# One hybrid transformer layer on eight cores: reciprocal square roots as exp(-0.5 ln x), and semaphore waits in place of pipeline drains

## The reference, cut to what matters

```python
x = x + attn_a(layernorm(x))      # differential attention, 8 heads, cosine logits
x = x + ffn(layernorm(x))         # x @ int4-like(kernel) + bias + (x @ a) @ b
x = x + attn_b(layernorm(x))      # 16 heads, RoPE, causal softmax
x = x + ffn(layernorm(x))

def layernorm(x): return (x - mean(x)) / sqrt(var(x) + 1e-5)
def l2norm(t):    return t / maximum(norm(t, axis=-1), 1e-6)
# attn_a, per head; q1, q2, k1, k2 are 64 wide, v 128 wide
L1 = l2norm(q1) @ l2norm(k1).T * cos_scale
L2 = l2norm(q2) @ l2norm(k2).T * cos_scale
G  = tanh(delta_gain * (L1 - L2))
y  = (softmax(L1 + G) - lambda_full * softmax(L2 - G)) @ v
y  = y * rsqrt(mean(y * y) + 1e-5) * subln_weight * 0.5
```

## Time and profile before

| what | value |
|---|---|
| median of 3 runs | 7120.11 us (7112.32 to 7128.64) |
| the profiled execution's own time | 7132.85 us |
| its span, slowest core (7) | 7131.2 us; the cores 7099.8 to 7131.2 |
| mean granted TensorE clock, by core | 0.605 to 0.609 of full speed |
| busy, share of the span | PE 40%, DVE 43%, ACT 19%, POOL 5% |

### The profile page before, as it was taken

The page is one execution under the profiler, slowest core; times in us unless marked ns, Lnnn a source line. Parts: engine busy times, 40 slices in busy tenths (PEclk is TensorE's granted clock), DMA queues, the critical chain, the costliest instruction groups (busy, mean ns, idle before and its releaser), DMA issues.

```text
span 7131.2 us, 34446 instructions; the slowest of 8 cores (7099.8 to 7131.2 us)
## 1 busy us (share of the span) xinstructions
PE 2824.4 (40%) x8352; PEld 684.9 (10%) x8352; DVE 3100.4 (43%) x3605; ACT 1389.2 (19%) x1544; POOL 358.5 (5%) x655
## 2 busy tenths in 40 slices
PE   0013011065656542030265656551505564565615
PEld 0000000010101000000010101010101111111201
DVE  1334525335555545435145555534145344444341
ACT  0000000033444330000044444410000242033100
POOL 0100010100000000000000000000000000000000
PEclk9975555555555555555555555565857666766758
DMA  2000000000000000000000000000000000000001
GB/s 79 25 12 18 1 21 2 12 13 6 6 6 6 6 11 10 6 17 1 23 5 6 6 6 6 6 27 12 13 25 24 14 6 15 25 5 6 26 12 60
DMA packets 129374, 104.56 MB, mean 15 GB/s; under 512 B 62078, under 2 KB 111486, under 8 KB 126878
## 3 DMA queue, kind: packets, MB, share of 16 engines
q1 hardware_dynamic: 81726, 65.43, 3.0%
q0 software_dynamic: 47456, 36.93, 2.1%
HBM read 90.85 MB, written 11.11 MB: 14 GB/s over the span
## 4 chain that ended last, share of the span: by engine, by line
DVE 31%; DMA 22%; PE 19%; issue 12%; ACT 10%; DVEq 6%; ACTq 0%; POOLq 0%; SPq 0%; PEldq 0%
DVE a_pL L102 6%; PE pj_p L102 6%; DVEq L102 6%; DVE rrow L102 5%; DMA rnb<-scrb 4%; ACT a_E L102 4%; ACT a_G L102 4%; DVE rrbq L102 3%; PE f_p L102 2%; DVE tmpf L102 2%; DMA b_rb<-scrb 2%; DVE a_rrb L102 2%; DMA wqb<-qout 2%; PE tm_pv L102 2%; DMA rrow<-scr 2%
## 5 line engine op out<-in xcount | busy, mean ns | idle before, releaser
L102 DVE TENSOR_TENSOR a_pL<-a_pL,a_G 128x512 f32<-128x512 f32 x1024 | 664.3, 694 | 978.4 <-ACT a_G L102 956.7
L102 PE MATMUL a_pY<-a_E,aV 128*128 128x512 bf16 x1024 | 518.8, 610 | 747.0 <-ACT a_E L102 747.0
L102 ACT ACTIVATE a_E<-a_pL,ccol 128x1024 bf16<-128x1024 f32 x512 | 570.6, 1114 | 1119.4 <-DVE a_pL L102 1119.1
L102 PE MATMUL pj_p<-xnA,pj_wb 128*128 128x512 bf16 x512 | 210.0, 585 | 837.6 <-DVE pj_wb L102 837.6
L102 ACT ACTIVATE b_E<-b_pS,ccol 128x1024 bf16<-128x1024 f32 (+1 forms) x320 | 312.1, 985 | 753.2 <-PE b_pS L102 751.5
L102 ACT ACTIVATE a_G<-a_pD,gvec 128x512 bf16<-128x512 f32 x512 | 348.6, 681 | 87.3 <-PE a_pD L102 87.3
L102 ACT ACTIVATE rrow<-rrow 1x1024 f32<-1x1024 f32 x64 | 67.5, 1055 | 1499.2 <-DMA rrow<-scr 1499.2
L102 PE MATMUL a_pD<-aQ,aKn 128*128 128x512 bf16 x512 | 307.9, 601 | 67.0 <-ACT rrow L102 49.8
L102 PE MATMUL tm_pv<-tm_wvh,xnA 128*128 128x512 bf16 x256 | 59.7, 398 | 683.2 <-DVE tm_wvh L102 683.2
L102 PE MATMUL a_pL<-aQ,aK 64*128 64x512 bf16 x1024 | 310.3, 603 | 2.8 <-DVE aV L102 2.8
L102 ACT ACT_TABLE_LOAD x69 | 88.5, 1283 | 1115.5 <-PE a_pD L102 390.9
(11 more groups left out here) (145 smaller groups left out, 3372.3 us busy)
## 6 DMA issues: line engine op xcount, KB each, us to landing
resid<-xT SPq DMA_DIRECT2D x8, 1024.0 KB
qf<-fker SPq DMA_DIRECT2D x16, 512.0 KB
rnb<-scrb POOLq DMA_DIRECT2D x64, 128.0 KB, 4.9
a_rb<-scrb POOLq DMA_DIRECT2D x32, 256.0 KB, 3.6
pj_wf<-WqkT SPq DMA_DIRECT2D x32, 256.0 KB
out<-resid SPq DMA_DIRECT2D x8, 1024.0 KB, 10.2
pj_wf<-WqT SPq DMA_DIRECT2D x16, 256.0 KB
bbR<-scr POOLq DMA_DIRECT2D x16, 256.0 KB, 3.4
```

The lines of the kernel that those rows point to most:

```text
L102: r = getattr(eng, name)(*args, **kw)
```

## The change

Two things change. First, `1/sqrt(x)` is made otherwise in two places: in the LayerNorm row (16 steps) and in the norm step (64 steps). ScalarE now takes `AF.Ln` and then `AF.Exp` with scale -0.5 in place of `AF.Sqrt`, and DVE's reciprocal goes; the guard becomes a minimum with 1e6. For K, where the reciprocal also wrote the bfloat16 row, a `tensor_copy` writes it now. The reciprocals of the softmax sums (`a_rrb`, `b_rrb`) and the `Sqrt` inside the scores loop stay.

Second, `Builder.drain` no longer emits a DRAIN. It makes the instruction ahead increment the engine's own semaphore (`s_dv` for DVE, `s_ds` for ScalarE) and waits for it; if that instruction increments a semaphore already it waits for that one, and after a wait it emits nothing. The program holds 1705 DRAINs before and 10 after, the wait instructions go from 9811 to 12346, and the NOPs from 189 to 997. The 808 new NOPs come from `drain` followed by `inc_last` on DVE: the instruction's increment is taken by `s_dv`, so `inc_last` adds a second wait and a NOP. In the program as it is built for the chip ScalarE's stream holds 69 table loads before and 69 after, and none of those after stands between an `Ln` and its `Exp`.

```diff
--- before.py
+++ after.py
@@ -69,8 +69,25 @@
         v = self.cnt[sem] if val is None else val
         self.ops[eng].append(("wait_ge", (self.sem_handles[sem], v), {}, []))
 
+    OWN_SEM = {"sync": "s_dn", "vector": "s_dv", "scalar": "s_ds",
+               "tensor": "s_dt", "gpsimd": "s_dg"}
+
     def drain(self, eng):
-        self.ops[eng].append(("drain", (), {}, []))
+        for entry in reversed(self.ops[eng]):
+            if entry[0] == "wait_ge":
+                return
+            if entry[0] in ("drain", "nop"):
+                continue
+            if entry[3]:
+                s0, _ = entry[3][0]
+                self.wait(eng, s0)
+                return
+            own = self.OWN_SEM[eng]
+            k = 16 if entry[0] == "dma_start" else 1
+            self.cnt[own] += k
+            entry[3].append((own, k))
+            self.wait(eng, own)
+            return
 
     def inc_last(self, eng, sem, k=1):
         for entry in reversed(self.ops[eng]):
@@ -183,7 +200,8 @@
 
     for s in ("s_ld", "s_pe", "s_ve", "s_se", "s_gd", "s_out", "s_bar",
               "s_lm", "s_dm", "s_g", "s_pa", "s_x", "s_pv", "s_ev", "s_sq",
-              "s_cons", "s_wc", "s_sr"):
+              "s_cons", "s_wc", "s_sr",
+              "s_dn", "s_dv", "s_ds", "s_dt", "s_dg"):
         b.sem(s)
 
     def sb(name, shape, dtype, stack=None):
@@ -443,11 +461,12 @@
             b.drain("vector")
             b.inc_last("vector", "s_ve")
             b.wait("scalar", "s_ve")
-            A.activation(rrow[0:1, QT:2 * QT], rrow[0:1, QT:2 * QT], AF.Sqrt,
-                         bias=ccol[0:1, 0:1], inc="s_se")
+            A.activation(rrow[0:1, QT:2 * QT], rrow[0:1, QT:2 * QT], AF.Ln,
+                         bias=ccol[0:1, 0:1])
+            b.drain("scalar")
+            A.activation(rrow[0:1, QT:2 * QT], rrow[0:1, QT:2 * QT], AF.Exp,
+                         scale=-0.5, inc="s_se")
             b.wait("vector", "s_se")
-            V.reciprocal(rrow[0:1, QT:2 * QT], rrow[0:1, QT:2 * QT])
-            b.drain("vector")
             V.tensor_mul(rrow[0:1, 0:QT], rrow[0:1, 0:QT], rrow[0:1, QT:2 * QT])
             b.drain("vector")
             b.inc_last("vector", "s_ve")
@@ -627,19 +646,19 @@
                     ld(G, rrow[0:1, 0:2 * QT],
                        d_scr[a_rn + g * 2 * QT:a_rn + (g + 1) * 2 * QT], sem="s_gd")
                     b.wait("scalar", "s_gd")
-                    A.activation(rrow[0:1, 0:2 * QT], rrow[0:1, 0:2 * QT], AF.Sqrt,
-                                 inc="s_se")
+                    A.activation(rrow[0:1, 0:2 * QT], rrow[0:1, 0:2 * QT], AF.Ln)
+                    b.drain("scalar")
+                    A.activation(rrow[0:1, 0:2 * QT], rrow[0:1, 0:2 * QT], AF.Exp,
+                                 scale=-0.5, inc="s_se")
                     b.wait("vector", "s_se")
-                    V.tensor_scalar_max(rrow[0:1, 0:2 * QT], rrow[0:1, 0:2 * QT], 1e-6)
+                    V.tensor_scalar_min(rrow[0:1, 0:2 * QT], rrow[0:1, 0:2 * QT], 1e6)
                     b.drain("vector")
                     if with_c:
-                        V.reciprocal(rrow[0:1, 0:2 * QT], rrow[0:1, 0:2 * QT])
-                        b.drain("vector")
                         V.tensor_scalar_mul(rrbq[0:1, 0:2 * QT],
                                             rrow[0:1, 0:2 * QT],
                                             cvec8[0:1, 4 * hg + mloc:4 * hg + mloc + 1])
                     else:
-                        V.reciprocal(rrbq[0:1, 0:2 * QT], rrow[0:1, 0:2 * QT])
+                        V.tensor_copy(rrbq[0:1, 0:2 * QT], rrow[0:1, 0:2 * QT])
                     b.drain("vector")
                     b.inc_last("vector", "s_ve")
                     b.wait("gpsimd", "s_ve")
```

## The result

The changed kernel takes 6891.8 us (median of 8 runs, 6885.7 to 6906.8) against 7120.1 us before. The ratio is 0.9683, with a 95% interval of 0.9672 to 0.9694, so 226 us less. I had forecast 6874 us, and 6790 to 6970 as the range. The direction, the mechanism and the range held; the forecast gain was 246 us, 20 too many.

The account below looks back on a forecast made before the run. No engine being more than half busy, a chain of hand-overs was taken to bound the kernel. Terms -168 - 144 - 35 + 15 + 86 = -246 us against the 7120.11 us median gave 6874 us, range 6790 to 6970.

Parts of the forecast that it names:

- No cover in the norm steps and the LayerNorm row: In these 80 serial steps everything removed or added counts in full: -168 us (Q), -144 (K), -35 (LayerNorm).
- The price of a copy: Norm step of K: the new copy to bfloat16 taken as 0.68 us; the other end, 1.21, costs 17 us more.
- What replaces a drain: Behind DVE instructions: a wait costs 0.10 us, a swap 0.025 more than a drain; a hand-over through a NOP 0.18.
- The rest of the hand-overs and swaps: Outside the 80 steps: about 600 plain swaps cost +15 us and 506 hand-overs on the chain +86 us.
- the 64 hand-overs behind the `pssq` copies: In A's projections: covered by PE's eight matmuls, so free; 0.17 us each if that cover were gone.
- the 74 hand-overs in the FFNs: On the chain, as PE waits for each `resid` update, `lora` or cast; 0.17 us each.
- the sum of hand-overs and swaps with those inside the steps: Whole kernel: the waits and NOPs in place of drains cost 123 us, at 0.17 a hand-over and 0.025 a swap.
- The clock: Rival, FFNs and B's projections: longer PE waits lower TensorE's clock, costing 76 and perhaps 25 us; 6975 us, chance 0.10.
- Free hand-overs: Extreme of the cheap hand-overs rival, whole kernel: swaps and hand-overs cost nothing, 6751 us; cheap hand-overs have chance 0.14.
- Table changes: Rival, 80 `Ln`/`Exp` pairs: each makes two table loads of 1.283 us, 205 us in all; 7079 us, chance 0.03.
- The dear NOP: Rival, 602 hand-overs on the chain: each costs 0.57 us more, 343 us; 7217 us, slower than before; chance 0.03.

Follow-up runs that it names:

- second profile of the changed kernel: The changed kernel, no code differing, run once more beside the kernel with real drains on one chip: ratio 0.9679.
- waits only: The kernel before with only `Builder.drain` changed, waits and NOPs in place of DRAINs, all `Sqrt` and reciprocals kept: 7263.6 us, ratio 1.0188.
- real drains: The changed kernel with `Builder.drain` emitting a DRAIN again, so only the reciprocals are exchanged: 6762.1 us, ratio 0.9480; once more on one chip, 0.9484.
- four more waits: The changed kernel with four more copies of the same wait in front of each of the 808 NOPs: 7096.0 us, ratio 0.9956.

## Why the prediction was right, step by step

- *No cover in the norm steps and the LayerNorm row.* Right. The gain by stage is 310.0 and 35.7 us; forecast were 312 and 35. The price of a copy that the trace of before did not have, between 0.68 and 1.21, came out at the end that I took, 0.681.
- *What replaces a drain.* The gap of 0.10, the hand-over's 0.17 to 0.18 and its anatomy (own wait, second wait, NOP) stand in the changed trace as forecast. They could be read before the run, because the kernel had this sequence once, behind `qsq`.
- *The rest of the hand-overs and swaps.* Forecast were +101 us outside the two rows. The median core's trace has -244.8 + 310.0 + 35.7 = +100.9, and +106 in the second profile of the changed kernel. The fit to a tenth is luck, and so in part is the sum, since single terms miss both ways. The scores of A got 27.0 us longer, where 124 x 0.17 is 21. A's projections got 7.0 us longer, where I had put the 64 hand-overs behind the `pssq` copies at nothing: at every fourth tile, in front of new weights, such a copy stands on the chain (at 656.68 in the trace of before). B's projections got 7.8 us longer, where 96 x 0.17 is 16: their matmuls ran at the higher clock told above. And 16 of the 74 hand-overs in the FFNs are covered by the DMA of the weights, while the clock cost about 6 us there.
- *Where the 20 us went.* The profiled execution's span fits the forecast (-244.8 us on the median core, -242.3 on the slowest), but the timed runs show 226 us less. The term of the forecast that is too small is the sum of hand-overs and swaps with those inside the steps, 123 us: the ratios show 134 (waits only), 139 and, between the two first series of runs, 145. The exchange alone is at 370 where I had 369. That the profiled pair fits is in part chance: its median cores were 4 and 8 us below the means of their kernels over all recorded executions (7111.1 against 7114.8, 6866.3 against 6873.8). By these means, too, the waits and NOPs cost more than 123: 134 (waits only) and 137 (changed kernel against real drains on one chip). So the mis-sized term is their price, by 10 to 20 us. A second part is the spread of the cores, which the forecast left alone: over all recorded executions the slowest core, which sets the time, lies 10 us above the median core before and 14 to 18 us above it in the changed kernel. The clock is no single answer, since it costs some 6 us in the FFNs and gives time back in B's projections. Which places make up the price beyond 123 us is known only by stage, as above.
- *The rivals.* Free hand-overs (the rule of the Trainium skill's "VectorE: DVE Perf Modes", section "The DRAIN you can't avoid", that a semaphore costs nothing extra) would have given 6751 us. That time belongs to the kernel that has real drains, 6762. Here the waits cost: little where the wait stands in a drain's place (23 us over the program), and much where it stands in front of a NOP that others wait for. Table changes did not occur, and in the 64 norm steps alone would have cost 151 to 177 us. The dear NOP, 0.59 us and more for a hand-over beyond the instruction's own increment, is excluded by the FFN, where it is 0.18 (0.32 against 0.14). The clock fell little in the change (0.87 to 0.84 in the FFN, and it rose in B's projections), and clearly with four more waits.

## What to carry to other kernels

In a chain of hand-overs, price an edit by its instructions' durations in full, and price the synchronization that comes with it in the same way: a hand-over that goes through a wait and a NOP instead of the producing instruction itself cost about 0.18 us, and 600 of them took back 92 to 122 of the 370 us that 80 removed reciprocals gave. Put the increment for the other engine on the instruction that makes the data, and let the same semaphore serve as the engine's own fence. On a single row, look at the shape before the function: the reciprocal costs by its columns, so two rows in different partitions belong in one instruction.

## What the runs showed of the hardware that was not expected

- A reciprocal takes 3.34 us for 512 columns in 1, 33 or 65 partitions, and 6.54 us for 1,024 columns in one; an activation of 1,024 columns takes 1.055 us.
- A wait that is met already costs DVE's sequencer 0.07 us on the chain, and 0.09 to 0.10 us if it waits for the instruction just ahead, against 0.075 for a DRAIN.
- With the gaps between the FFN's tiles 0.18 us longer its matmuls went from 440 to 452 ns in the mean, and with 0.46 us longer gaps to 492: more of the tiles of eight then take 3.57 us (1.2 GHz) and not 1.89 (2.4 GHz). In B's projections the same 0.18 us in the hand-overs brought the mean from 500 down to 454 ns, and four more waits brought it up to 537.
- A table load costs its 1.283 us and 0.02 to the activation, wherever the step is serial, also when it stands behind a long wait for a DMA: it begins only when that DMA has landed.
